# Fetching embedding rows for one more slot per pair of steps by single-row copies, from straight code

## What is computed

```python
x = jax.nn.relu(dense @ Wb0 + bb0)            # 13 -> 512
x = jax.nn.relu(x @ Wb1 + bb1)                # 512 -> 256
d = jax.nn.relu(x @ Wb2 + bb2)                # 256 -> 64
sp = emb[jnp.arange(26)[None, :], sparse_idx] # 26 rows of 64 float32 per sample
T = jnp.concatenate([sp, d[:, None, :]], axis=1)
Z = jnp.einsum('bnd,bmd->bnm', T, T)
inter = Z[:, li, lj]                          # the 351 pairs below the diagonal
h = jnp.concatenate([d, inter], axis=1)
h = jax.nn.relu(h @ Wt0 + bt0)                # 415 -> 512
h = jax.nn.relu(h @ Wt1 + bt1)                # 512 -> 256
p = jax.nn.sigmoid(h @ Wt2 + bt2)
```

## Time and profile before

| | us |
|---|---|
| median of 3 runs (lowest, highest) | 537.01 (536.68, 538.55) |
| the profiled execution | 538.77 |
| its span in the trace | 536.8 |
| GpSimd busy | 379.5 (71%) |
| TensorE matmuls busy | 308.3 (57%) |
| VectorE busy | 245.0 (46%) |
| ScalarE busy | 13.7 (3%) |

### The profile page before, as it was taken

One profiled execution on the slowest core, in us unless ns is written; L12 is line 12 of the kernel. 1 busy time (PEld: TensorE's weight loads), 2 busy tenths in 40 slices (PEclk: granted clock), 3 DMA queues, 4 the chain that ended last, 5 costly groups with the idle time before them and its releaser, 6 DMA issues.

```text
span 536.8 us, 12271 instructions
## 1 busy us (share of the span) xinstructions
PE 308.3 (57%) x3370; PEld 226.9 (42%) x3370; DVE 245.0 (46%) x375; ACT 13.7 (3%) x23; POOL 379.5 (71%) x406
## 2 busy tenths in 40 slices
PE   2999973764371643744447344583436633596667
PEld 1333333652260522723236242473226522594655
DVE  5445676645462523743257332585247334513111
ACT  1000000000000000000000000000000000021201
POOL 5777777777777777777777777777777777477700
PEclk9996897685576755677667675587558675687677
DMA  6454424443354433444254433444334443223300
GB/s 198 39 28 29 28 30 29 29 30 30 27 32 28 29 28 28 30 31 26 28 28 27 29 29 27 30 27 29 28 29 28 30 26 28 18 24 28 28 9 1
DMA packets 19968, 16.88 MB, mean 31 GB/s; under 512 B 11683, under 2 KB 12972, under 8 KB 19897
## 3 DMA queue, kind: packets, MB, share of 16 engines
q0 software_dynamic: 12800, 13.13, 31.3%
q1 hardware_dynamic: 4378, 2.68, 4.5%
q10 hardware_dynamic: 2732, 0.51, 3.4%
HBM read 16.28 MB, written 0.01 MB: 30 GB/s over the span
## 4 chain that ended last, share of the span: by engine, by line
POOL 34%; PE 22%; DMA 17%; issue 16%; DVE 9%; POOLq 0%; ACT 0%; DVEq 0%; ACTq 0%
POOL rows L307 34%; DMA rows<-in_emb,idx_step 16%; PE ps_t L343 6%; PE ps_gram L397 4%; DVE vecs_mv L702 3%; PE ps_t L477 2%; PE ps_turn L365 2%; PE ps_turn L351 2%; PE ps_t L446 1%; PE ps_feat L334 1%; PE ps_gram L334 1%; DVE gram_s L712 1%; PE ps_feat L446 1%; DVE gram_s L714 1%; DVE vecs_st L702 1%
## 5 line engine op out<-in xcount | busy, mean ns | idle before, releaser
L307 POOL DMA_INDIRECT rows<-in_emb,idx_step x400 | 377.9, 945 | 131.4 <-issue 123.1
L365 PE MATMUL ps_turn<-ident,rows 128*128 128x128 f32 x182 | 41.2, 369 | 148.4 <-DMA rows<-in_emb,idx_step 139.8
L702 DVE COPY vecs_st<-ps_turn 128x512 f32<-128x512 f32 (+1 forms) x49 | 46.9, 958 | 119.6 <-PE ps_turn L365 119.2
L702 DVE COPY vecs_mv<-ps_turn 64x512 f32<-64x512 f32 (+1 forms) x98 | 96.1, 981 | 0.7
L365 PEld LDWEIGHTS ps_turn<-ident,rows 128*128 128x128 f32 x182 | 27.3, 185 | 163.4 <-issue 155.6
L397 PE MATMUL ps_gram<-vecs_mv,vecs_st 128*32 128x54 f32 x1792 | 41.6, 282 | 32.7 <-DVE vecs_mv L702 19.5
L397 PEld LDWEIGHTS ps_gram<-vecs_mv,vecs_st 128*32 128x32 f32 x1792 | 38.6, 161 | 37.1 <-DVE vecs_mv L702 22.3
L477 PE MATMUL ps_t<-wt_sb,ht_t 128*128 128x256 f32 x128 | 51.8, 575 | 0.0
L477 PEld LDWEIGHTS ps_t<-wt_sb,ht_t 128*128 128x128 f32 x128 | 35.2, 288 | 14.7 <-issue 7.8
L712 DVE STREAM_TRANSPOSE gram_s<-ps_gram 128x864 f32<-128x864 f32 x16 | 17.3, 1083 | 52.2 <-PE ps_gram L397 40.2
L446 PE MATMUL ps_t<-feat_t,wt_sb 117*128 117x128 f32 x192 | 37.8, 352 | 0.6 <-ACT feat_t L587 0.6
(11 more groups left out here) (57 smaller groups left out, 229.0 us busy)
## 6 DMA issues: line engine op xcount, KB each, us to landing
fetched<-in_emb SPq DMA_DIRECT2D x1024, 0.2 KB
fetched<-in_emb ACTq DMA_DIRECT2D x1024, 0.2 KB
rows<-in_emb,idx_step POOLq DMA_INDIRECT x400, 3.6
wt_sb<-in_wt SPq DMA_DIRECT2D x1, 1024.0 KB
wb_sb<-in_wb SPq DMA_DIRECT2D x1, 512.0 KB
wt_sb<-in_wt SPq DMA_DIRECT2D x1, 512.0 KB
idx_raw<-in_idx SPq DMA_DIRECT2D x1, 175.0 KB, 3.0
wt_sb<-in_wt ACTq DMA_DIRECT2D x1, 128.0 KB
```

The source lines that it names most:

```text
L307: nc.gpsimd.indirect_dma_start(rows[:, t, h * DIM:(h + 1) * DIM], None, emb_rows, bass.IndirectOffsetOnAxis(idx_step[:, c:c + 1], 0)).then ...
L365: turned = nc.tensor.transpose(ps_turn[r % 2][:, j, :], rows[:, first + j, :], ident[:, :])
L702: moved = nc.vector.tensor_copy(to, source)
```

## The change

Five slots per pair of steps are copied row by row in place of four: the two slots of table 25 in the even step, and in the odd step these and half 1 of table 24. Each slot is now shared: SP copies its rows 0 to 63 and ACT its rows 64 to 127, in two parts each. So each queue has 4 parts in an even step and 6 in an odd one, 40 parts (1280 copies) in place of 32 (1024). The loop over pairs is written out. GpSimd leaves out the gather of table 24, half 1, in odd steps: 396 gathers in place of 400. In even steps that gather raises a semaphore of its own, `even_gathered`, for which the even step's `move_fetched` waits. In the last half step the runs are reordered so that tables 20 and 21 are gathered and turned last, and the move of the fetched rows is split by halves. The staging of runs 4 to 6 (`stage_rest`) stands before `spread(i, 6)`, no longer in `products`.

```diff
-FETCHED = TABLES - 1
-GATHERED = [min(n, FETCHED - t) for t, n in RUNS]
+GATHERS = TABLES - 1
+GATHERED = [min(n, GATHERS - t) for t, n in RUNS]
+LANDED = [32 * n for n in GATHERED[:NR - 1]] + [16]
+
+
+LAST_RUNS = [RUNS, RUNS[:NR - 2] + [(TABLES - 4, 4), (TABLES - 6, 2)]]
+LAST_GATHERED = [GATHERED, [n for _, n in RUNS[:NR - 2]] + [2, 2]]
 
 HEAD = 4
 HEAD_COLS = 2 * RUNS[HEAD][0]
-STEP_COLS = 2 * FETCHED
+STEP_COLS = 2 * GATHERS
 
 
 ROW_BYTES = 4 * DIM
-PARTS = 4
-PART = P // PARTS
+PART = 32
+PAIRS = STEPS // 2
+
+
+FETCH_SLOTS = ((TABLES - 1, 0, 0), (TABLES - 1, 0, 1), (TABLES - 1, 1, 0), (TABLES - 1, 1, 1), (TABLES - 2, 1, 1))
+EVEN_SLOTS, ODD_SLOTS = (0, 1), (2, 3, 4)
+SLOT_PLACE = (0, 4, 8, 12, 32)
+FETCH_PARTS = SLOT_PLACE[-1] + 4
...
+        def load_places(engine, queue, slot, part, k):
+
+            p = SLOT_PLACE[slot] + 2 * queue + part
...
-            with sp.Fori(0, STEPS // 2) as k:
-                for side in range(2):
-
-                    sp.wait_ge(fetched_moved, k * 2 + (side + 1))
-                    for q in range(PARTS):
-                        places = load_places(mybir.EngineType.SP, 0, q, k * 2 + side)
-                        for j in range(PART):
-                            sp.dma_start(landing(side, 0, q * PART + j), emb_bytes[bass.ds(places[j], ROW_BYTES)])\
-                                .then_inc(fetch_landed[0][side][q // 2], 16)
+            sp.wait_ge(fetch_done, 5)
+            def fetch(slot, k):
+                for part in range(2):
+                    places = load_places(mybir.EngineType.SP, 0, slot, part, k)
+                    for j in range(PART):
+                        sp.dma_start(landing(slot, part * PART + j),
+                                    emb_bytes[bass.ds(places[j], ROW_BYTES)]).then_inc(fetch_landed[slot][0], 16)
...
+            for k in range(PAIRS):
+
+                sp.wait_ge(fetched_moved, k * 2 + 1)
+                for slot in EVEN_SLOTS:
+                    fetch(slot, k)
+
+                sp.wait_ge(fetched_moved, k * 2 + 2)
+                for slot in ODD_SLOTS:
+                    fetch(slot, k)
...
-            with pool.Fori(0, STEPS - 1) as i:
+            def step(i, odd):
                 for staged, lo, hi in parts:
                     begin(i, staged, hi)
                     for r in range(lo, hi):
                         first = RUNS[r][0]
                         for t in range(first, first + GATHERED[r]):
                             for h in range(2):
-                                gather(t, h, rows_landed[r])
+                                if (t, h) != (TABLES - 2, 1):
+                                    gather(t, h, rows_landed[r])
+                                elif not odd:
+                                    gather(t, h, even_gathered)
+
+            with pool.Fori(0, PAIRS - 1) as k:
+                step(k * 2, False)
+                step(k * 2 + 1, True)
+            step(STEPS - 2, False)
...
-                if r == NR - 1:
-                    pe.wait_ge(fetched_moved, STEPS + 2)
+                pe.wait_ge(rows_landed_last[h][r], 16 * LAST_GATHERED[h][r])
+                if first + n == TABLES:
+                    pe.wait_ge(fetched_moved, STEPS + h + 2)
...
-            def move_fetched(i, side, nth):
-
-                for h in range(2):
-                    for q in range(PARTS // 2):
-                        dve.wait_ge(fetch_landed[h][side][q], nth * (32 * PART))
+            def move_fetched(i, odd, nth):
+
+                for slot in (ODD_SLOTS if odd else EVEN_SLOTS):
+                    for queue in range(2):
+                        dve.wait_ge(fetch_landed[slot][queue], nth * (16 * 2 * PART))
                 dve.wait_ge(rows_turned, i * NR + NR)
-                nc.vector.tensor_copy(rows[:, FETCHED, :], fetched[:, side, :]).then_inc(fetched_moved, 1)
+                if odd:
+                    moved = nc.vector.tensor_copy(rows[:, TABLES - 2:, :].rearrange("p t c -> p (t c)")[:, DIM:], fetched_odd[:, :])
+                else:
+
+                    dve.wait_ge(even_gathered, nth * 16)
+                    moved = nc.vector.tensor_copy(rows[:, TABLES - 1, :], fetched_even[:, :])
+                moved.then_inc(fetched_moved, 1)
...
+            def move_fetched_last(h):
+
+                for slot in (ODD_SLOTS[:1], ODD_SLOTS[1:])[h]:
+                    for queue in range(2):
+                        dve.wait_ge(fetch_landed[slot][queue], PAIRS * (16 * 2 * PART))
+                dve.wait_ge(rows_turned, (STEPS - 1) * NR + NR)
+                if h == 0:
+                    moved = nc.vector.tensor_copy(rows[:, TABLES - 1, 0:DIM], fetched_odd[:, DIM:2 * DIM])
+                else:
+                    nc.vector.tensor_copy(rows[:, TABLES - 2, DIM:], fetched_odd[:, 0:DIM])
+                    moved = nc.vector.tensor_copy(rows[:, TABLES - 1, DIM:], fetched_odd[:, 2 * DIM:])
+                moved.then_inc(fetched_moved, 1)
...
+            def stage_rest(i):
+                stage(i, rest_staged, HEAD_COLS, STEP_COLS, range(HEAD, NR))
...
-                stage(i, rest_staged, HEAD_COLS, STEP_COLS, range(HEAD, NR))
                 move_feat(i, 1)
...
                 copy_d(i)
-                move_fetched(i, side, nth)
+                move_fetched(i, odd, nth)
                 spread(i, 5)
+                stage_rest(i)
                 spread(i, 6)
                 products(i)
```

More of the change, by code:

```diff
@@ L179, in build @@
         fetch_done = sem("fetch_done")
-        fetch_landed = [[[sem(f"fetch_landed{h}_{side}_{q}") for q in range(PARTS // 2)] for side in range(2)]
-                        for h in range(2)]
+        fetch_landed = [[sem(f"fetch_landed{slot}_{queue}") for queue in range(2)] for slot in range(len(FETCH_SLOTS))]
+        even_gathered = sem("even_gathered")
         fetched_moved = sem("fetched_moved")
@@ L233, in turned_half @@
         def turned_half(h, r):
-            first, n = RUNS[r]
+            first, n = LAST_RUNS[h][r]
             part = slice(DIM * h, DIM * (h + 1))
@@ L246, in load_places, with landing @@
             return places
-        def landing(side, h, p):
-            return fetched[p:p + 1, side, h * DIM:(h + 1) * DIM].bitcast(U8)
+        def landing(slot, p):
+            to, first = ((fetched_even, 0), (fetched_even, 1), (fetched_odd, 1), (fetched_odd, 2), (fetched_odd, 0))[slot]
+            return to[p:p + 1, first * DIM:(first + 1) * DIM].bitcast(U8)
         def unrolled_pairs(u):
@@ L324, in _ @@
                     for r in range(lo, hi):
-                        first = RUNS[r][0]
-                        for t in range(first, first + GATHERED[r]):
+                        first = LAST_RUNS[h][r][0]
+                        for t in range(first, first + LAST_GATHERED[h][r]):
                             gather(t, h, rows_landed_last[h][r])
@@ L624, in _, with fetch @@
             nc.scalar.activation(probs[:, 0:1], ones[:, 0:1], ACT.Sigmoid).then_inc(table_ready, 1)
-            act.wait_ge(fetch_done, 4)
-            with act.Fori(0, STEPS // 2) as k:
-                for side in range(2):
-                    act.wait_ge(fetched_moved, k * 2 + (side + 1))
-                    for q in range(PARTS):
-                        places = load_places(mybir.EngineType.Activation, 1, q, k * 2 + side)
-                        for j in range(PART):
-                            act.dma_start(landing(side, 1, q * PART + j), emb_bytes[bass.ds(places[j], ROW_BYTES)])\
-                                .then_inc(fetch_landed[1][side][q // 2], 16)
+            act.wait_ge(fetch_done, 5)
+            def fetch(slot, k):
+                for part in range(2):
+                    places = load_places(mybir.EngineType.Activation, 1, slot, part, k)
+                    for j in range(PART):
+                        act.dma_start(landing(slot, (2 + part) * PART + j),
+                                     emb_bytes[bass.ds(places[j], ROW_BYTES)]).then_inc(fetch_landed[slot][1], 16)
+            for k in range(PAIRS):
+                act.wait_ge(fetched_moved, k * 2 + 1)
+                for slot in EVEN_SLOTS:
+                    fetch(slot, k)
+                act.wait_ge(fetched_moved, k * 2 + 2)
+                for slot in ODD_SLOTS:
+                    fetch(slot, k)
             act.wait_ge(d_ready, CHUNKS)
@@ L764, in first_step, with step @@
                     spread(0, 2 * (c - FIRST_CHUNKS) + 3)
-                move_fetched(0, 0, 1)
+                move_fetched(0, False, 1)
+                stage_rest(0)
                 spread(0, NR - 1)
                 products(0)
-            def step(i, side, nth):
+            def step(i, odd, nth):
                 spread(i, 0)
@@ L801, in last_step @@
                 spread_last(1, 2)
+                move_fetched_last(1)
                 spread_last(1, 4)
@@ L835, in _ @@
                     dve.wait_ge(fetch_done, 2)
```

(10 more changed lines are left out.)

32 lines of the change are left out of this document (16 added, 16 removed).

## The result

The changed kernel takes 593.01 us (median of 4 runs, 590.95 to 593.56), the kernel before 537.78 (4 runs, 536.68 to 539.39). The ratio is 1.102, with a 95% interval of 1.098 to 1.106. The profiled execution took 593.16 us, its span is 591.4. The forecast was 583.

A forecast was written before the change was run, and what follows sets the result against it. ScalarE's copies were taken to hold its last step: copies end 524.4, plus 2.1, 54.0 and 1.8 gives a span of 582.3; 2.0 outside it makes 584.3, less 1.8 for the median, near 582.5, stated as 583 us. Range 565 to 597.

The forecast's parts named there:

- What bounds it: ScalarE's last step stands in its program behind its copies, so the whole last step starts when they end, at 524.4.
- The end of the copies: On ACT's queue: start 6.5, eight parts of 13.14 us, 32 of 12.91, less 0.3, giving 524.4 us.
- The bounds (513.0 to 531.8): End of ACT's copies if each part costs what SP's do (12.67 us), or if all cost 13.14.
- wait for a landing buffer: On ACT's queue: none stretches the copies; the fetched rows' move comes near 397 us, the fill needing it at 447.
- The tail: After the copies: 2.1 us to TensorE's sum, 54.0 to the end, 1.8 for the clock; 57.9 us of span.
- the 1.8 us added for it: TensorE starts the last step out of idleness at a lower clock: one sum's difference, 1.8 us, bounds 0 and 4.
- The gain of the staging: On GpSimd: indices staged earlier on VectorE, so the break of 5.90 us in the last step goes, -5.6 us.
- four fewer gathers: On GpSimd: four gathers of 1.25 us each go, -5.0 us.
- The landings: Rival, 0.14: copies land ever later behind their issue, so the last landing sets the end, 586 to 598 us.
- Quicker issue: Rival on the copy queues: straight code shortens parts; partly, 545 to 570 us, 0.14; until GpSimd bounds, 528 us, 0.04.
- the worse supply of instructions: Rival, 0.05: straight code brings breaks of 2.9 us every eight parts (+11.6) to every two (+58), 596 to 640 us.
- the likeliest case: ScalarE's copies set the end as summed, chance 0.60; its own range 571 to 593 us.

The follow-up runs named there:

- the six parts on ScalarE and on SP: Kernel before plus 192 extra copies into unused memory after a queue's own copies: 577.08 us on ScalarE ahead of its last step, 540.85 on SP.
- the kernel without ScalarE's last step: Changed kernel with all of ScalarE's part of the last step moved into VectorE's program: 582.39 us, ratio 1.080.

## Why the prediction was right, and where it was off

*What bounds it.* Right. ScalarE's copies set the start of the last step: the chain is 75% ACT's queue, the wait of TensorE for `vecs_act` is 32 us, and the six parts on ScalarE and on SP tell the place from the amount (577.1 against 540.9 us).

*The end of the copies.* Forecast 524.4, measured 533.7: this is the term that was mis-sized, by 9.3 us of the 10 that the forecast was short. The tail gave back 0.2, and 0.9 lie outside the span: the forecast had put the median 0.7 us above it, and it came 1.6 above. By its own steps: the first eight parts came as summed (111.3 against 111.6). The other 32 were put at the 12.91 us of the loop's later turns; in the changed kernel they are 13.06, together +4.9 (with only straight code 13.09). And of the last ten, nine came at 13.47 on average and the last took 13.8, another +4.7. The working had taken the lower price from the loop's later turns and at the same time dropped the loop; written out, the copies of this kernel keep the price of the first turn. That it is straight code as such is not shown: the 192 written-out copies behind the loop, on ScalarE, took 224 ns each and (505.3 - 441.7)/5 = 12.72 us per part. The bounds (513.0 to 531.8) did not hold it either, since the highest row, 13.14, had been taken for the most a part can cost. No wait for a landing buffer came, as forecast: the move of step 5 stood at 426.75 us in place of 397, still 26 us ahead of ScalarE's load at 452.9 that needs it.

*The tail.* Forecast 57.9 us of span behind the copies, measured 591.4 - 533.7 = 57.7. Its pieces: 3.4 to TensorE's sum in place of 2.1, then 54.3 in place of 55.8. That the whole fits to 0.2 us is luck in part, since these two misses cancel. The first came because a matmul of 1.22 us (L497), which the working had left out, stands on TensorE between ScalarE's relu and the sum. In the second, the sum took 3.78 us, as it does at the 1.2 GHz level, and the 1.8 us added for it were there. But over the whole stretch from that sum to the end TensorE was busy only 0.8 us longer than before, and its other waits were shorter. First before, then after (length; busy PE, PEld, DVE, ACT, POOL; granted clock, DMA):

```profile
476.20:536.80 60.60, 41.79 (x693) 35.12 (x692) 12.12 (x24) 9.70 (x16) 26.89 (x29) 0.75 0.20 18
...
537.10:591.40 54.30, 42.63 (x693) 36.75 (x692) 12.05 (x24) 9.19 (x16) 0.00 (x0) 0.73 0.03 2
```

The clock over the stretch was nearly the same, 0.75 and 0.73. Only its beginning differs: 0.77 in the 18 us after ScalarE's start, against the 0.91 of the earlier trace rows.

```profile
534.00:552.00 18.00, 16.06 (x268) 12.94 (x271) 3.16 (x8) 5.23 (x10) 0.00 (x0) 0.77 0.08 3
```

*GpSimd.* The gain of the staging is real by itself (-5.5 us); that of four fewer gathers (forecast -5.0) was not run by itself. Neither reached the time. In the changed kernel GpSimd ends 13.4 us later than before, since its waits for indices rose from 8.4 to 27.4 us. At 427 us the rows show the cause, the copies' landings by way of VectorE's move; for the other waits it is argued from there. `even_gathered` held nothing up for long: one wait of 6.6 us for gathers at 208 us, far ahead of the end.

*The rivals.* The landings grow as the steeper of the two rates had it (0.057 per us, forecast 0.04, rival 0.06), and the last copies, in the kernel without ScalarE's last step, lag 22 us, less than the 28 at 399 us. There the landings set 582 us, 11 us under ScalarE, so they were hidden, but only just. The result lies inside the 586 to 598 us that had been given to the landings, for another reason. Quicker issue did not come; the loads got slower by 3%, the DMA instructions by 5% against the loop's later turns. Nor did the worse supply of instructions as it was priced: a pause of 2.9 us every eight parts would have shown, and ScalarE's longest DMA instruction before 360 us took 518 ns. Two figures of the working are off by its own terms and change nothing: the lower end of the likeliest case is 583 - 13.2 = 570 and not 571, and one such pause every eight parts gives 595 and not 596.

*Branches, issue and transfer engines.* Straight code showed no pause of the loop's size (12.9 us from the eighth to the ninth load), and the loop's first two turns showed pauses of 2.9 and 2.8 us. The rule of the Trainium skill on a taken branch ("Runtime: NRT & Kernel Launch", Instruction fetch mechanics) agrees with that; that the pause is a fetch of instructions, no run here shows. The copies of 64 bytes took their queue as long as those of 256. The Trainium skill says that initiating a DMA is usually small beside the DMA itself ("DMA: Bandwidth & Descriptors", Issuing engines are not separate DMA queues), and for one copy the trace agrees: 0.26 us of issue against 13 to 28 us until it has landed. That the copies would hide because of it does not follow, since the issue of 1280 of them adds up on the queue while their landings overlap.

The prediction also read a rule of the Trainium skill ("DMA: Bandwidth & Descriptors", Why a DMA increments its semaphore by 16 and not by 1) more widely than it stands: the Trainium skill goes by the slowest dimension whose size is not 1, and its own example of a copy of few bytes on one engine is of a single element. The counts of packets on the profile's pages fit the prediction's reading as far as they go. The 192 extra copies on ScalarE added 384 packets to its queue (3116 against 2732), two for each, so a row is not cut into 16; in two pieces it makes four (5804 against 3244 for 1280 copies). Which engine carries them, no run shows.

## What to carry to other kernels

A queue's issue time is a resource that the busy shares do not show: count copies per queue (here 13 us for 32 register-addressed ones, with 64 bytes each as with 256), and look at what stands behind them in the same engine's program before adding any. Put such work on the queue behind which nothing waits. When an engine's waits shrink by moving one instruction, take that edit by itself (here -1.1%); bundled with one that delays what the instruction now stands behind, it gave nothing.

## What had not been expected of the hardware

A single-row copy in two pieces costs 637 ns per DMA instruction in place of 235, and a part of 32 as much as two parts of whole rows. The same instructions are a little slower written out than in a loop from its second turn on (loads 2.25 against 2.18 us, copies 235 against 224 ns), but copies written out behind the loop took 224 ns again; what makes the difference was not found. Near the end of both queues single copies pause by up to 0.9 us: the longest DMA instruction of ACT is 879 ns in the row below. These pauses came after 360 us in the changed kernel and in all four of its versions that copy each row in one piece on both queues in full. With four slots, in straight code, there was none, so their place in time alone does not make them. Copies land 13 us behind their issue at 137 us and 28 us at 399 us, with 256 bytes each and with 64. The cause of the last two was not found.

```profile
L661 ACTq DMA_DIRECT2D fetched_odd<-in_emb x768: 234/235/879, 61.0 to 533.5; - x192
```
